# Two VectorE steps of a fused attention and feed-forward kernel as three-operand instructions

## The reference

```
ln(x) = (x - mean) / sqrt(var + 1e-5)

x = x + A(ln(x)):  Q, K, V = sigmoid(4 * (batchnorm(x @ W) - 1))
                   t_Q = 1 - mean(Q), t_K = 1 - mean(K)        # one number for a token
                   delta = t_Q - t_K^T                         # 256 x 256
                   f = 0.9 * exp(-2 * |delta|)
                   S = where(delta < 0, f, -f) + 0.9
                   A = S @ V @ Wo + bo
x = x + F(ln(x)):  silu(x Wg) * (x Wu), times Wd, 384 hidden units, integer weights
x = x + B(ln(x)):  causal softmax attention, 16 heads of 64
x = x + F(ln(x)):  the same feed-forward block
```

## Time and profile before

| | |
|---|---|
| median of 3 executions | 340.31 us (340.23 to 340.88) |
| the profiled execution, its own time | 340.77 us |
| its span, first to last instruction | 338.7 us |
| TensorE busy | 319.7 us, 94% |
| VectorE busy | 269.0 us, 79% |
| ScalarE busy | 231.5 us, 68% |
| GpSimd busy | 198.5 us, 59% |
| TensorE's granted clock | 1.000 |

### The profile page before, as it was taken

One profiled execution on the slowest core, in us unless ns is written; L12 is line 12 of the kernel. 1 busy time (PEld: TensorE's weight loads), 2 busy tenths in 40 slices (PEclk: granted clock), 3 DMA queues, 4 the chain that ended last, 5 costly groups with the idle time before them and its releaser, 6 DMA issues. The chain is left out here.

```text
span 338.7 us, 9997 instructions
## 1 busy us (share of the span) xinstructions
PE 319.7 (94%) x3264; PEld 278.0 (82%) x3264; DVE 269.0 (79%) x1092; ACT 231.5 (68%) x784; POOL 198.5 (59%) x265
## 2 busy tenths in 40 slices
PE   2888999999999998999999999999999999999995
PEld 2767788889888977889988888889988878888875
DVE  4468799988987889878979879878787897967645
ACT  2643678876688858576887757777868738787811
POOL 4585456778745657947566197742757186355600
PEclk9999999999999999999999999999999999999999
DMA  7900000000000000000000000000000000000001
GB/s 194 296 0 3 1 2 4 2 1 3 2 2 2 2 2 3 15 3 3 2 16 4 2 2 1 18 2 0 4 17 0 3 3 17 3 0 3 3 15 33
DMA packets 6418, 5.83 MB, mean 17 GB/s; under 512 B 864, under 2 KB 5856, under 8 KB 6368
## 3 DMA queue, kind: packets, MB, share of 16 engines
q1 hardware_dynamic: 6080, 4.99, 5.0%
q10 hardware_dynamic: 288, 0.20, 0.2%
HBM read 4.15 MB, written 1.05 MB: 15 GB/s over the span
## 5 line engine op out<-in xcount | busy, mean ns | idle before, releaser
L908 POOL TENSOR_TENSOR prob<-prob,row_inv 128x256 f32<-128x256 f32 (+1 forms) x128 | 102.6, 828 | 87.7 <-DVE row_inv L814 87.7
L640 ACT ACTIVATE prob<-neg_s,neg_max 128x128 f32<-128x128 f32 x128 | 50.7, 396 | 24.5 <-DVE neg_max L799 23.6
L642 ACT ACTIVATE prob<-neg_s,neg_max 128x256 f32<-128x256 f32 x128 | 63.7, 498 | 0.0
L799 DVE CUSTOM_DVE_ANT_0 neg_s<-bank,mask 128x256 f32<-128x256 f32 x128 | 53.6, 419 | 0.0
L536 PE MATMUL bank<-prob_t,v 128*64 128x256 f32 (+1 forms) x512 | 48.5, 332 | 0.9 <-DVE ntk L727 0.7
L824 DVE TENSOR_TENSOR qk<-bank,bqk 128x512 f32<-128x512 f32 x64 | 42.6, 682 | 3.6 <-PE bank L352 3.6
L536 PEld LDWEIGHTS bank<-prob_t,v 128*64 128x64 f32 x512 | 32.9, 136 | 15.4 <-issue 4.9
L797 DVE CUSTOM_DVE_ANT_0 neg_s<-bank,mask 128x128 f32<-128x128 f32 x128 | 36.5, 285 | 10.5 <-PE bank L501 9.6
L650 ACT ACTIVATE prob_t<-bank 128x384 f32<-128x384 f32 x64 | 29.6, 482 | 14.7 <-PE bank L513 14.4
L501 PE MATMUL bank<-qk 64*128 64x256 f32 x256 | 39.0, 377 | 0.0
L350 PE MATMUL bank<-rt_hi,wqkv_hi 128*128 128x256 f32 x128 | 38.8, 303 | 0.2 <-DVE neg_max L799 0.2
(11 more groups left out here) (146 smaller groups left out, 786.3 us busy)
## 6 DMA issues: line engine op xcount, KB each, us to landing
wqkv<-wqkv_in SPq DMA_DIRECT2D x3, 512.0 KB, 6.9
x<-x_in SPq DMA_DIRECT2D x8, 128.0 KB, 5.8
out<-x SPq DMA_DIRECT2D x8, 128.0 KB, 1.8
wo<-wo_in SPq DMA_DIRECT2D x1, 512.0 KB, 7.0
wa<-wa_in ACTq DMA_DIRECT2D x1, 192.0 KB, 3.0
wg_i<-wg_in SPq DMA_DIRECT2D x1, 192.0 KB, 3.3
wu_i<-wu_in SPq DMA_DIRECT2D x1, 192.0 KB, 3.4
wd_i<-wd_in SPq DMA_DIRECT2D x1, 192.0 KB, 5.3
```

Of the source, the lines that this page charges most:

```text
L640: nc.scalar.activation(prob[:, r, e, 0:P], neg_s[:, m % 2, e, 0:P], ACT.Exp, bias=neg_max[:, q, 2 * e:2 * e + 1], scale=-1.0, accum_out=ro ...
L642: nc.scalar.activation(prob[:, r, e, P:SC], neg_s[:, m % 2, e, P:SC], ACT.Exp, bias=neg_max[:, q, 2 * e + 1:2 * e + 2], scale=-1.0, accum_ ...
L799: nc.vector.tensor_tensor_reduce(out=neg_s[:, m % 2, e, P:SC], in0=S[:, P:SC], in1=mask[:], scale=-SCORE_SCALE, scalar=3e38, op0=ALU.add, ...
L908: nc.gpsimd.tensor_tensor(pr, pr, inv, ALU.mult).then_inc(p_norm, 1)
```

## The change

Two lines of VectorE's program are written with another instruction. Line 702 added epsilon with a `tensor_scalar`, which has one tensor input. It becomes a `scalar_tensor_tensor` with the variance as both of its tensor inputs: max(var + epsilon, var), which is var + epsilon. Line 732 compared with a `tensor_scalar` against the constant 0. It becomes a `scalar_tensor_tensor` whose second tensor input is the zero half of `mask`, read twice over, once for each half of the 256 columns. As it reads `mask`, the first `mean` job waits until GpSimd has filled the constants. Orders and banks, and all else, are as they were.

```diff
@@ lnsX: epsilon, 32 instructions @@
-                    nc.vector.tensor_scalar(var[c][:], mv[c][:, :, 1], EPS, None, ALU.add).then_inc(var_s[k], 1)
+                    nc.vector.scalar_tensor_tensor(var[c][:], mv[c][:, :, 1], EPS, mv[c][:, :, 1], ALU.add, ALU.max).then_inc(var_s[k], 1)
@@ mean: comparison, 16 instructions @@
                     full(dve, job, b)
+                    if b == 0:
+                        dve.wait_ge(consts_in, 4)
...
                     for j in range(T):
-                        last = nc.vector.tensor_scalar(less[:, j, :], tq[:, b % 2, :], ntk[:, b % 2, j:j + 1], 0.0, ALU.add, ALU.is_lt)
+                        last = nc.vector.scalar_tensor_tensor(less[:, j, :].rearrange("p (k s) -> p k s", s=P), tq[:, b % 2, :].rearrange("p (k s) -> p k s", s=P),
+                                                              ntk[:, b % 2, j:j + 1], mask[:, 0:P].unsqueeze(1).to_broadcast([P, T, P]), ALU.add, ALU.is_lt)
```

## The result

The changed kernel takes 341.70 us (median of 6, 341.50 to 342.57), the kernel before 340.27 (6 runs): a ratio of 1.0044, with a 95% interval of 1.0031 to 1.0058. It is slower, by 1.4 us. The forecast was 340.9 us with a range to 341.8, so the measured time lies 0.1 us inside the range, and the change is two and a half times the forecast one. The profiled execution took 341.67 us, its span is 339.6.

The account below looks back on a forecast made before the run. TensorE was busy 319.7 of 338.7 us, so VectorE's edits count only where TensorE waits for it. Batches 0, 1 and 4 add 0.02 + 0.27 + 0.27 = 0.56 us to 340.31: 340.9 us, range 339.4 to 341.8.

Parts of the forecast that it names:

- Held starts: Epsilons and comparisons on VectorE that wait for GpSimd: all 20 held starts stay as they are, change 0.
- The comparison's length: Line 732's comparison on VectorE: 353 ns becomes 488 (426 if the operand is free), 0.27 us for each `mean` job.
- Batches 1 and 4 come through, 0, 6 and 7 don't: Longer comparisons reaching TensorE: 0.27 us each in batches 1 and 4, 0.02 in batch 0, 0 in 6 and 7.
- Five gaps of TensorE behind held starts: TensorE's waits at lines 442, 498, 536 and two at 513: 3.7 us together, unchanged if starts stay held.
- rival (2): The new form isn't held beside GpSimd, so TensorE's five gaps close: 337.2 us; chance 0.08.
- Batches 2, 3 and 5: VectorE's later idle time covers the longer comparison: 0 counted for each, 0.27 us each as upper bound.
- Rival (1): More batches' longer comparisons reach TensorE, up to 0.27 us each; priced at two more batches, 341.4 us; chance 0.28.
- Rival (4): Longer comparisons shift later epsilons against GpSimd, so other pairs collide; one lost hold of 0.8 gives 340.1 us; chance 0.20.

## Why the prediction was right, and where it was short

- **Held starts: right.** The new form with two SBUF inputs waits for GpSimd as the old one does. The forecast was 0 for 32 epsilons, measured 0.03 us. The Trainium skill ("SBUF — State Buffer", section "Who interferes with whom") says that a VectorE instruction with two SBUF inputs contends with a GpSimd one that reads SBUF, that a `tensor_scalar` in a two-port mode can contend too, and that a `tensor_reduce` doesn't, nor an instruction with at most one SBUF input outside those modes. These runs agree: both forms of the epsilon were held, up to 1.05 us, while no reduction took above 159 ns and no comparison from PSUM above 485. By that section of the Trainium skill, whoever issues first has the shared pair of ports "for the whole instruction"; by the earlier trace rows the held instruction starts 0.13 to 0.15 us before the recorded end of GpSimd's. Recorded spans on GpSimd are rough, so whether this is the engine's or the record's I haven't shown.
- **The comparison's length: right.** 488 ns were forecast from rows of other instructions, 485 measured; 0.27 us a batch, against five jumps of 0.26.
- **Batches 1 and 4 come through, 0, 6 and 7 don't: right.** The prediction had 0.02 us for batch 0; no jump shows there.
- **Five gaps of TensorE behind held starts: one too few.** The prediction's list lacks the 0.57 us at 22.65, behind the epsilon held at 21.17. As the held starts stayed, this cost the forecast nothing; rival (2) it made too cheap, and the reduction gained 0.71 us there.
- **Batches 2, 3 and 5: wrong.** This is the step that failed: "so 0.27 us fit in each", and from it "I count 0 for all". It is the term that was mis-sized: with three batches at nothing the sum was 0.56 us, for a measured 1.4. Rival (1) was true, at three batches more, not the two at which it was priced; with three its own arithmetic gives 341.7 us. That the time lies in the range is owed to this rival, whose price set the upper bound. The outcome held likeliest, a change within 0.2% at 0.45, did not come; the kernel is 0.44% slower, and slower stood at 0.41. In batch 2 the idle time covered VectorE's own queue, but not what GpSimd had been asked for behind the comparison. In batches 3 and 5 the idle time came too late: a job ahead of it was already the one for which TensorE waited.

That last point could be read in the trace of the kernel before. VectorE's copy behind comparison 3 and its mask behind comparison 5 in the kernel before, and TensorE's instructions that wait for them:

```profile
94.40 0.55 DVE L807 COPY prob_t<-bank 128x384 f32<-128x384 f32 x1
```

```profile
95.10 0.40 PE L513 MATMUL bank<-ident,prob 64*128 64x64 f32 x6
```

```profile
171.58 0.41 DVE L799 CUSTOM_DVE_ANT_0 neg_s<-bank,mask 128x256 f32<-128x256 f32 x1
```

```profile
172.16 0.50 PE L350 MATMUL bank<-wqkv_hi,rt_hi 128*128 128x512 f32 x1
```

The copy ends at 94.95 and TensorE starts at 95.10; the mask ends at 171.99 and TensorE starts at 172.16. In the changed kernel the same pair stands 0.15 us apart with an idle time in brackets:

```profile
172.40 0.41 DVE L802 CUSTOM_DVE_ANT_0 neg_s<-bank,mask 128x256 f32<-128x256 f32 x1
```

```profile
172.96 0.47 PE L350 MATMUL bank<-wqkv_hi,rt_hi 128*128 128x512 f32 x1 [0.19 <-DVE neg_max L802]
```

The last semaphore for which either of TensorE's instructions waited was that of this copy and of this mask; the others had come at least 3 us earlier. So those starts were already set by VectorE, with no slack. No gap was printed because the matmuls ahead of them end only at 95.24 and 172.23 in the trace, and the ends of matmuls are modelled. I took the lack of a gap for slack.

The longer comparison does hold GpSimd in its turn, as the prediction thought possible: of the two `xn` instructions of 0.80 us each beside the comparison of batch 3, the first took 0.98 us in the kernel before and 1.26 in the changed one. No jump of TensorE can be put down to this.

Rival (4), other pairs colliding, hardly occurred: the same 15 epsilons are held in both kernels, and four of the five comparisons; the fifth, in batch 6, had been held for 0.11 us and no longer is, and no gap of TensorE followed it in either. Rival (2), unheld starts, was out for this form of instruction, but its price was sound in kind: the reduction, which isn't held, gives 2.5 us by the medians, and 2.7 by its ratio.

## What to carry to other kernels

Where one engine is busy for 94% and its orders are fixed, don't read slack from the lack of a gap: look, for each of its starts, at how long before it the awaited instruction ended. In batches 2, 3 and 5 of this kernel starts 0.10, 0.15 and 0.17 us behind their releaser had none. Idle time of the edited engine covers a delay only if nothing ahead of it, or on another engine that it feeds, is awaited. And an instruction of a few numbers that is held beside GpSimd can cost its queue most of GpSimd's instruction (0.88 us for 2 numbers here): writing it as one that isn't held, a reduction over a constant column, made this kernel 0.8% faster, while alone the old instruction takes 0.17 us and the reduction 0.16.

## What the runs showed of the hardware

- A `tensor_reduce` of 2 x 2 SBUF numbers took 156 to 159 ns in all 32 cases, 15 of them in jobs whose one-input or three-operand form had been held beside GpSimd and had taken up to 1.05 us. A `tensor_scalar` whose columns come from PSUM took 474 to 485 ns in all 20 cases of two kernels.
- On 256 columns in float32, with one operand for each partition, the one-input form from SBUF takes 353 ns, the three-operand form 485 and the one-input form from PSUM 480. A repeated read of the second input is free (485 both ways).
- What is gained by freeing one instruction of a hold can be lost at the next: in the kernel with batches 1 and 4 from PSUM the copy behind the comparison was held in its place (1.44 us for a copy of 0.68). It need not be so: freeing the epsilons gave 2.5 us.
- What GpSimd does counts. In the kernel before, a comparison at 170.00 and an epsilon at 198.41 came during GpSimd's power of 2 columns (from 169.89 to 170.66, and from 198.37 to 199.09) and took 341 and 170 ns: neither was held. A `sign` at 133.57 and an epsilon at 277.23 came 0.23 and 0.20 us after the start of a GpSimd `xn` of 0.80 us, and with the times that they take alone they were let go 0.30 us after that start, not near its end; the comparison at 203.53, beside another `xn`, 0.60 us after its start.
